# Shared-expert products between the routing logits, and a second attention that takes its operands in order of need, on one core

## The reference

```python
# first MoE (xt: the layer-normed tokens)
scores = sigmoid(xt @ gate.T)                       # 8 experts
_, sel = top_k(scores + expert_bias, 2)             # two of eight, each weighted by its score
routed expert e: silu(xb @ w1[e].T) * (xb @ w3[e].T) @ w2[e].T     # xb: bf16 of score * xt
shared expert:   silu(xt @ sw1.T) * (xt @ sw3.T) @ sw2.T           # f32, all tokens
# second attention (h: the layer-normed tokens, m: the context)
scores = einsum('bsd,bmd->bsm', h, m) / sqrt(256)
scores = where(mask, scores, -1e30)
out = softmax(scores) @ m
```

## Time and profile before

| | |
|---|---|
| median of 3 runs | 3015.5 us (3014.59 to 3016.41) |
| the profiled execution | 3013.14 us, of which its span is 3011.3 us |
| PE busy | 95% of the span |
| DVE, ACT, POOL busy | 69%, 66%, 56% |
| first MoE | 2447 to 2596 us of the span |
| second attention | 2597 to 2810 us of the span |

### The profile page before, as it was taken

The page is one execution under the profiler, slowest core; times in us unless marked ns, Lnnn a source line. Parts: engine busy times, 40 slices in busy tenths (PEclk is TensorE's granted clock), DMA queues, the critical chain, the costliest instruction groups (busy, mean ns, idle before and its releaser), DMA issues. The chain is left out here.

```text
span 3011.3 us, 58598 instructions
## 1 busy us (share of the span) xinstructions
PE 2865.1 (95%) x18733; PEld 2451.1 (81%) x18733; DVE 2089.1 (69%) x4511; ACT 1993.3 (66%) x4950; POOL 1686.2 (56%) x2119
## 2 busy tenths in 40 slices
PE   7989999799999999999999999999999998699698
PEld 5768888688888888888888888888888875488655
DVE  7974455677777777777777777777777768656544
ACT  5656666677777777777777777777777639666211
POOL 6766663456556555655655565565556436465132
PEclk9999999999999999999999999999999989899699
DMA  5456767421111111111111111111111010354510
GB/s 182 136 159 205 209 205 220 137 68 55 41 68 42 54 41 69 54 41 68 43 53 41 68 54 41 68 44 52 41 68 54 1 48 1 106 153 125 179 42 26
DMA packets 249669, 253.40 MB, mean 84 GB/s; under 512 B 12470, under 2 KB 225599, under 8 KB 249376
## 3 DMA queue, kind: packets, MB, share of 16 engines
q1 hardware_dynamic: 229856, 228.92, 23.4%
q10 hardware_dynamic: 17312, 15.73, 1.8%
q0 software_dynamic: 2208, 5.12, 0.6%
HBM read 165.71 MB, written 84.93 MB: 83 GB/s over the span
## 5 line engine op out<-in xcount | busy, mean ns | idle before, releaser
L1027 ACT ACTIVATE w_hi<-ps_t 128x512 fp32r<-128x512 f32 (+2 forms) x1024 | 569.9, 557 | 415.3 <-PE ps_t L1267 412.0
L1097 DVE TENSOR_REDUCE piece_max<-ps_s 128x1 f32<-128x512 f32 (+2 forms) x1024 | 631.8, 623 | 257.4 <-PE ps_s L1254 229.7
L1123 DVE TENSOR_TENSOR w_lo<-ps_t,w_hi 128x512 fp32r<-128x512 f32 (+2 forms) x1024 | 656.4, 641 | 200.0 <-ACT w_hi L1027 183.7
L1287 PE MATMUL ps_o<-w_hi,v_hi 128*128 128x256 f32 (+1 forms) x1856 | 595.8, 321 | 0.0
L1194 POOL TENSOR_SCALAR prob<-prob,inv_sum 128x512 f32<-128x512 f32 (+2 forms) x768 | 477.3, 641 | 195.7 <-DVE inv_sum L1113 195.7
L1289 PE MATMUL ps_o<-w_hi,v_lo 128*128 128x256 f32 (+1 forms) x1856 | 523.5, 282 | 0.0
L1288 PE MATMUL ps_o<-w_lo,v_hi 128*128 128x256 f32 (+1 forms) x1856 | 522.3, 281 | 0.0
L1015 ACT ACTIVATE prob<-ps_s,neg_max 128x512 f32<-128x512 f32 (+2 forms) x768 | 487.3, 635 | 44.0 <-DVE neg_max L1104 35.2
L1267 PE MATMUL ps_t<-ident,prob 128*128 128x128 f32 (+1 forms) x2784 | 515.8, 272 | 0.0
L1249 PE MATMUL ps_s<-k_hi,q_hi 128*128 128x512 f32 (+2 forms) x1024 | 403.7, 394 | 27.6 <-ACT prob L1015 18.3
L1267 PEld LDWEIGHTS ps_t<-ident,prob 128*128 128x128 f32 (+1 forms) x2784 | 359.7, 140 | 52.4 <-issue 0.2
(11 more groups left out here) (291 smaller groups left out, 6208.4 us busy)
## 6 DMA issues: line engine op xcount, KB each, us to landing
v_scratch<-v_out SPq DMA_DIRECT2D x120, 256.0 KB, 3.0
raw_k<-k_scratch SPq DMA_DIRECT2D x32, 960.0 KB
raw_v<-v_scratch SPq DMA_DIRECT2D x32, 960.0 KB
k_scratch<-k_out SPq DMA_DIRECT2D x104, 256.0 KB, 2.7
q_scratch<-out_t SPq DMA_DIRECT2D x64, 256.0 KB, 2.5
r_all<-r_scratch SPq DMA_DIRECT2D x32, 512.0 KB
raw_q<-q_scratch SPq DMA_DIRECT2D x32, 512.0 KB
first_prob<-in_ctx_t ACTq DMA_DIRECT2D x50, 256.0 KB, 2.8
```

What stands on the lines that cost most here:

```text
L1027: nc.scalar.activation(pt_hi[keys, k % RING, cols], ps_t[keys, k % 2, cols], ACT.Copy).then_inc(hi_done, 1)
L1097: nc.vector.tensor_reduce(piece_max[:, n % 2, p:p + 1], ps_s[:, p, lo - p * PC:hi - p * PC], AX.X, ALU.max).then_inc(max_ready, 1)
L1123: nc.vector.tensor_tensor(pt_lo[keys, k % RING, cols], ps_t[keys, k % 2, cols], pt_hi[keys, k % RING, cols].bitcast(F32), ALU.subtract).th ...
L1287: nc.tensor.matmul(out, v_hi[gi][keys, vs], pt_hi[keys, k % RING, cols], start=blk == (0 if qt else 1), stop=False)
```

## The change

In the first MoE the shared expert's bursts 0, 1 and 2 are issued behind the logits of pairs 1, 3 and 5, and burst 3 behind the last logits. Turned tiles go to two banks in place of four; one of them is later `ps_b`. The tanh of each burst stands on ACT between the copies, and on DVE the first three `shared_silu` and `shared_gated` stand ahead of `choose()`.

In the second attention `pen` and `row0` have one partition in place of 128, and the memset of `pen` covers 2 x 63 elements of one partition; the three memsets that are left stand ahead of `norm_rstd`. Two `xt_hi` on ACT and the low parts on DVE are interleaved in the order in which the first scores want them, and these scores wait for one piece at a time. On DVE the row maxima of units 0 and 1 now stand ahead of `norm_mean_var` of parts 1 to 3.

```diff
@@ first MoE, scalar
+                    if g % 2 == 1 and g >= 3:
+                        half_tanh(g // 2 - 1)
...
-                half_tanh(0)
-                half_tanh(1)
-                half_tanh(2)
                 half_tanh(3)
@@ first MoE, vector
+                for j in range(SHARED - 1):
+                    shared_silu(j)
+                    shared_gated(j)
                 dve.wait_ge(gate_loaded, 32)
                 choose()
-                dve.wait_ge(xt_copied, PAIRS)
-                for j in range(SHARED):
-                    shared_silu(j)
-                    shared_gated(j)
-                    if j >= 2:
-                        inputs(j - 2)
+                shared_silu(SHARED - 1)
+                shared_gated(SHARED - 1)
+                inputs(0)
+                inputs(1)
                 copy_h1(0)
@@ first MoE, tensor
-                    if g >= 4:
-                        pe.wait_ge(xt_copied, g - 3)
+                    if g >= 2:
+                        pe.wait_ge(xt_copied, g - 1)
...
-                    last.then_inc(logits, 1)
+                        if g == PAIRS - 1:
+                            last.then_inc(logits, 1)
+                        if g % 2 == 1 and g < PAIRS - 1:
+                            if g == 1:
+                                pe.wait_ge(sw_loaded, 48)
+                            shared_hidden(g // 2)
...
                 route()
-                pe.wait_ge(sw_loaded, 48)
-                shared_hidden(0)
-                shared_hidden(1)
+                shared_hidden(3)
+                inputs(0)
+                inputs(1)
                 pe.wait_ge(score_exps, 1)
-                shared_hidden(2)
-                inputs(0)
-                shared_hidden(3)
-                inputs(1)
                 pe.wait_ge(w_cast, 3 * E0)
                 hidden(0)
@@ second attention
-        pen = sb("pen5", [P, 2, KP], BF16)
-        row0 = sb("row0_5", [P, P], BF16)
+        pen = sb("pen5", [1, 2, KP], BF16)
+        row0 = sb("row0_5", [1, P], BF16)
@@ gpsimd
+                nc.gpsimd.memset(row0[:, :], 1.0).then_inc(row0_ready, 1)
+                nc.gpsimd.memset(prob[:, :, T:KP], 0.0).then_inc(zeroed, 1)
+                nc.gpsimd.memset(pen[:, :, T:KP], 0.0).then_inc(zeroed, 1)
                 norm_rstd(nc, pool, mean_var, rstd, half, norm, 0)
-                nc.gpsimd.memset(row0[:, :], 0.0).then_inc(row0_ready, 1)
-                pool.wait_ge(row0_ready, 1)
-                nc.gpsimd.memset(row0[0:1, :], 1.0).then_inc(row0_ready, 1)
-                nc.gpsimd.memset(prob[:, :, T:KP], 0.0).then_inc(zeroed, 1)
-                nc.gpsimd.memset(pen[:, :, :], 0.0).then_inc(zeroed, 1)
                 for part in range(1, NORM_PARTS):
                     norm_rstd(nc, pool, mean_var, rstd, half, norm, part)
@@ scalar
-                for x in range(4):
-                    split_t(0, 0, x)
-                for v in range(2):
-                    high_x(0, v)
+                split_t(0, 0, 0)
+                high_x(0, 0)
+                split_t(0, 0, 1)
+                high_x(0, 1)
+                split_t(0, 0, 2)
+                split_t(0, 0, 3)
@@ vector
-                dve.wait_ge(zeroed, 2)
+                low_t(0)
+                low_x(0, 0)
                 penalty(0, 0)
+                for x in range(1, len(PIECES)):
+                    low_t(x)
+                low_x(0, 1)
+                for p in range(SL):
+                    piece_maximum(0, 0, p)
+                negative_maximum(0, 0)
+                normalise(0, 2)
                 penalty(0, 1)
-                low_x(0, 0)
-                low_x(0, 1)
-                normalise(0, 2)
+                for p in range(SL):
+                    piece_maximum(0, 1, p)
+                negative_maximum(0, 1)
                 for part in range(1, NORM_PARTS):
                     norm_mean_var(nc, dve, x_sb, mean_var, norm, part)
                 scale_rstd(1, NORM_PARTS)
                 dve.wait_ge(scaled, 2)
-                for n in range(2):
-                    for p in range(SL):
-                        piece_maximum(0, n, p)
-                    negative_maximum(0, n)
                 low_x(0, 2)
@@ tensor
                         if n % 2 == 0:
-                            pe.wait_ge(tl_done, (i * 2 + n // 2 + 1) * 4)
+                            if not first:
+                                pe.wait_ge(tl_done, (i * 2 + n // 2 + 1) * 4)
                             pe.wait_ge(pen_ready, i * 2 + n // 2 + 1)
+                    if first:
+                        pe.wait_ge(tl_done, p + 1)
```

More of the change, by code:

```diff
@@ L1390, in moe_two_of_eight @@
         ps_y = psum("ps_y4", [P, 2, 512])
-        ps_b = psum("ps_b4", [P, 1024], BF16)
+        ps_turned = psum("ps_turned4", [P, 512])
+        ps_b = ps_turned[:, :].bitcast(BF16)
         pair_h1, pair_h3 = (ps_h1[:, :], ps_acc[:, 0, :]), (ps_h3[:, 0, :], ps_h3[:, 1, :])
-        turned = [ps_h1[:, :], ps_h3[:, 0, :], ps_h3[:, 1, :], ps_y[:, 1, :]]
+        turned = [ps_y[:, 1, :], ps_turned[:, :]]
         ps_logits = ps_y[:, 0, 0:NT * E0]
@@ L1451, in _ @@
             def _(act):
-                for g in range(PAIRS):
-                    act.wait_ge(xt_ready, g + 1)
-                    nc.scalar.activation(xt[:, :, g * 2 * P:(g + 1) * 2 * P].rearrange("p c (t n) -> p c t n", t=2),
-                                         turned[g % 4].rearrange("p (t c n) -> p c t n", t=2, c=DC), ACT.Copy).then_inc(xt_copied, 1)
-                act.wait_ge(logits, 1)
-                nc.scalar.activation(score_exp[:, :, :], ps_logits.rearrange("p (t e) -> p t e", t=NT), ACT.Exp, scale=-1.0).then_inc(score_exps, 1)
                 def half_tanh(j):
@@ L1464, in half_tanh @@
                     nc.scalar.activation(tanh[:, j % 2, :], pair_h1[j % 2], ACT.Tanh, scale=0.5).then_inc(tanh_ready, 1)
+                for g in range(PAIRS):
+                    act.wait_ge(xt_ready, g + 1)
+                    nc.scalar.activation(xt[:, :, g * 2 * P:(g + 1) * 2 * P].rearrange("p c (t n) -> p c t n", t=2),
+                                         turned[g % 2].rearrange("p (t c n) -> p c t n", t=2, c=DC), ACT.Copy).then_inc(xt_copied, 1)
+                    if g % 2 == 1 and g >= 3:
+                        half_tanh(g // 2 - 1)
+                act.wait_ge(logits, 1)
+                nc.scalar.activation(score_exp[:, :, :], ps_logits.rearrange("p (t e) -> p t e", t=NT), ACT.Exp, scale=-1.0).then_inc(score_exps, 1)
                 def copy_y(k, h):
@@ L1640, in turn, with shared_hidden @@
                             at = (t * DC + c) * P
-                            last = nc.tensor.transpose(turned[g % 4][:, at:at + P], xn[:, 2 * g + t, c * P:c * P + P], ident[:, :])
+                            last = nc.tensor.transpose(turned[g % 2][:, at:at + P], xn[:, 2 * g + t, c * P:c * P + P], ident[:, :])
                     last.then_inc(xt_ready, 1)
+                def shared_hidden(j):
+                    for m, (ps, done, free) in enumerate(((pair_h1, h1_ready, siluf_ready), (pair_h3, h3_ready, actf_ready))):
+                        if j >= 2:
+                            pe.wait_ge(free, j - 1)
+                        for c in range(DC):
+                            last = nc.tensor.matmul(ps[j % 2], sw[:, m, c * H0:c * H0 + H0], xt[:, c, j * N:(j + 1) * N], start=c == 0, stop=c == DC - 1)
+                        last.then_inc(done, 1)
                 def route():
@@ L1663, in inputs @@
                     last.then_inc(xbt_ready, 1)
-                def shared_hidden(j):
-                    for m, (ps, done, free) in enumerate(((pair_h1, h1_ready, siluf_ready), (pair_h3, h3_ready, actf_ready))):
-                        if j >= 2:
-                            pe.wait_ge(free, j - 1)
-                        for c in range(DC):
-                            last = nc.tensor.matmul(ps[j % 2], sw[:, m, c * H0:c * H0 + H0], xt[:, c, j * N:(j + 1) * N], start=c == 0, stop=c == DC - 1)
-                        last.then_inc(done, 1)
                 def hidden(k):
@@ L2008, in penalty @@
                         dve.wait_ge(scores_ready, (i * 2 + b - 1) * 2 * SL)
-                    nc.vector.tensor_scalar(pen[0:1, b % 2, 0:T], mask[0:1, b % 2, :], -NEG, NEG, ALU.mult, ALU.add).then_inc(pen_ready, 1)
+                    nc.vector.tensor_scalar(pen[:, b % 2, 0:T], mask[:, b % 2, :], -NEG, NEG, ALU.mult, ALU.add).then_inc(pen_ready, 1)
                 def piece_maximum(i, n, p):
@@ L2058, in _, with low_t @@
                 normalise(0, 1)
-                for x, (lo, hi) in enumerate(PIECES):
+                def low_t(x):
+                    lo, hi = PIECES[x]
                     dve.wait_ge(th_done, x + 1)
@@ L2121, in transpose_x, with scores @@
                     last.then_inc(xt_ready, 1)
-                def scores(i, n, p):
+                def scores(i, n, p, first=False):
                     b = (n // 2) % 2
@@ L2173, in _ @@
```

(5 more changed lines are left out.)

## The result

The changed kernel took 3050.42 us (median of 4 runs, 3048.47 to 3051.48) beside 3015.21 us (3014.59 to 3016.41) of the kernel before in the same job: a ratio of 1.0113, 95% interval 1.0099 to 1.0128. It is slower, as forecast, but by 35 us and not by 22.6, above the range of 3030 to 3046. The profiled execution took 3048.47 us with a span of 3046.7.

The account below looks back on a forecast made before the run. PE was taken to bound the second attention and ACT the first MoE's loop, so late starts pass on in full. MoE +4.5 and attention +18.1 gave +22.6 us: 3035.7 profiled, 3038 median, range 3030 to 3046.

Parts of the forecast that it names:

- The sign: Whole kernel: the change makes it slower, chance 0.95; same 0.04, faster 0.01.
- Rival (c): Second attention: POOL's late release is hidden, so not slower; 3017 us, no measurable change; chance 0.04.
- The first MoE: Routing and loop entry: last logits 7.8 us later, first routed product 3.3 us later; +4.5 us in all.
- clock kept: First MoE: PE's clock is not lost between bursts; low end of that stage's range, +2.3 us.
- The rule on transposes: First MoE routing: transposes don't count as PE-busy like products, so turns between bursts do nothing for the clock.
- rival (b): First MoE: clock lost in every light stretch, bursts 1 to 3 each pay 2.2 us; 3043 us; chance 0.11.
- The head start: Second attention opening: first scores about 3.5 us earlier, first exponential 2.9 us earlier, set by ACT's `r_hi`.
- The new wait: Second attention: POOL free 16.7 us later behind the second maximum; first product with the rows +16.2 us.
- The cold start: Second attention: PE's first dense work runs at half clock after the wait; +1.9 us, between 1.6 and 3.
- The failed step: Second attention: the penalty product's smaller height costs nothing; a tenth per pass would be 2.6 us either way.
- The range: Whole kernel: 3030 to 3046 us; the favoured case alone 3031 to 3045, chance 0.82.
- case (d): Second attention: batch 1 loads land sooner, exponential at 2615.5; 3035 us, 3031 with the MoE at best; chance 0.03.

Follow-up runs that it names:

- run 14: Not a follow-up run: in "had run 14 us", turns and logits ahead of the first burst took 14 us at 1.2 GHz.

## Why the prediction was wrong, step by step

- *The sign* holds, and by the mechanism named: without the term that failed the kernel is still 21.8 us slower. Rival (c) is out, as POOL's release came at 2637.64 and PE's start is released by `r_lo`.
- *The first MoE.* I had +4.5 us, measured +2.4 (its lower end was +2.3, "clock kept"). Taking off the 1.06 us of the later start, the last logits end at 2476.41 + 1.91 - 1.06 = 2477.3 where I had 2478.9: the clock was not lost between bursts, and the 2.2 us that I counted for one loss were not spent (without them I had 2476.7). From there to the first routed product it is 2490.40 - 2478.32 = 12.1 us, and I had 12.2. What follows costs 0.9 (the stage's 2.4 less the 1.5 by which the first routed product is late), and I had 1.2 for a slow start of the loop.
- *The rule on transposes* that I set beside this, from the Trainium skill, TensorE: Matmul & The Clock Gate, Part 4 (PE-mode transpose), was to cost more here: by it the turns do nothing for the clock. The trace doesn't bear that price out: turns together with narrow logits, 2.5 us between bursts, left PEclk at 1.00 from 2463 to 2486, so rival (b) is out. What turns alone would do no run shows.
- *The head start.* Right: the first scores start 4.1 us ahead in their stage (11.00 us against 15.13), where I had 3.6, and the exponential moved 2.99 us ahead in its stage (2621.83 - 2598.32 = 23.51 against 26.50), where I had 2.9, and it is set by ACT's `r_hi`. With the large memset put back it is at 23.49: once the maxima stand ahead, the memset does not matter. But the maxima are not all of the gain. With them behind the variances again the exponential still comes 2.1 us ahead (24.43), and with the large memset back as well 1.2 (25.26).
- *The new wait.* Right: POOL is free 39.32 us into the stage where it was 21.75, 17.6 later (I had 16.7); the first product with the rows is 16.95 us later (I had 16.2), and 15.95 with the penalty at 128 partitions; the 1.00 us between them is about what the penalty products of the second unit lose, whose scores stand on this path. The idle time I had wrong in kind: some 11 us, all ended by POOL. It is 10.93 + 8.69 us, and only the second is ended by POOL; that the first has my number is chance. It is the wait for DVE's `pt_lo`, which the forecast did not have and which cost nothing as long as POOL was later.
- *The cold start.* I had 1.9 us. The attention of the kernel with 128 partitions is 18.4 us longer, of which 15.95 lie ahead of the first product with the rows: 2.4 behind it, in my 1.6 to 3. Directly: from the first product with the rows to the end of the piece of scores behind it that kernel takes 5.57 us (2653.42 to 2658.99) where before takes 3.09, 2.5 us more. The slow start is all of it.
- *The failed step*, in the prediction's words: "The product of `row0` with `pen` keeps its 512 columns, and I cost its smaller height at nothing; were each of the stage's 64 longer or shorter by a tenth of the 0.40 us of such a pass, that would be 2.6 us either way." The pass did not get longer. Its neighbours lost their overlap with it: 0.26 to 0.29 us a full piece, some 0.23 a short one, 0.91 in the period of a unit, and 13.75 us in the stage (246.76 - 233.01). Two mistakes are in it: the bound was made from the duration of the pass, which cannot show what a change of height does to the passes beside it; and it was left out of the range that should have held it.
- *The range.* Two of its ends do not follow from the terms. The MoE's +8.6 is nowhere added up, and the lower 3031 is not reached: MoE at +2.3, cold start at 1.6 and 2 us for the exponential make 3033.5, and case (d) with the MoE at its best 2.2 less than 3035, 3032.8. Neither changes the outcome: the time lies above the range.

The account of the profiled execution: forecast 3035.7, MoE -2.1, attention +14.0 (32.1 - 18.1), later start of the MoE +1.1, together 3048.7; it took 3048.47. The later start is scatter and no effect of the change.

The Trainium skill, TensorEngine Tiling (Array Packing), Key Properties, has a rule that bears on this: changing the tiling mode, not just the tile, drains TensorE; and its Tiling Modes count 128 rows as no row tiling, 64 and 32 rows as the others. The trace agrees in that 1, 32 and 64 partitions cost 0.91 to 0.95 us a unit, 65 nothing, and a second product of the same height nothing beyond its columns. That it is this drain, and that a low product is put into such a mode without being asked, the runs suggest but do not show; heights between 65 and 128 were not run.

## What to carry to other kernels

Where PE is the bound, an operand's number of partitions is not free: a product over 1, 32 or 64 partitions between products over 128 costs 0.26 to 0.29 us for going in and out once (512 columns, 2.4 GHz), so either keep it above 64 by zero rows (65 and 128 were free here) or put such products side by side. Before moving a block on one engine's queue, list every engine that waits for anything behind it: the variances held up POOL and DVE itself, and removing only the longer wait gave back 9.3 of 17 us. Light work between dense bursts is cheap once a burst has raised the clock, but leave enough dense work behind the last result that others wait for: one burst more there was worth 4.6 us of stage, of which the medians show some 3 (1.9 above before with three bursts between, 1.2 below with two).

## What the runs showed of the hardware that I had not expected

A product over 1, 32 or 64 partitions delays the products over 128 beside it: 0.33 us instead of 0.23 ahead, 0.64 instead of 0.46 behind, at 2.4 GHz and 512 columns; over 65 it does not. PE is reported busy all of the time in both cases, so the busy share hides it; the same 659 products in 102.51 us against 95.19 show it, and so does the busy share of the weight loads, 80% against 86% (81.84 of 102.51 us, 81.72 of 95.19).

The granted clock stayed at 1.00 from 2463 to 2486 us, with turns and narrow logits between the bursts and with the first 4.1 us of the pause behind the last burst; in the kernel with two bursts on each side also through pauses of 2.09 and 1.20 us ahead of the routed inputs. Behind the whole pause of 5.83 us the first products ran at 0.50. The same turns and logits ahead of the first burst had run 14 us at 0.50 without a pause.
